# Three PSUM banks for both kinds of scores, a penalty written by ScalarE for every second head, and six batches' values made ahead of the feed-forward part

## The reference, cut to what matters

```python
# layer 0, attention; layer 1 is the same without the mask
Q = (layernorm(x) @ W_q.T) ; K = (ctx @ W_k.T) ; V = (ctx @ W_v.T)      # 16 heads of 16
scores = where(mask, Q @ K.T / sqrt(16), -1e10)                          # per head 256 x 256
x = x + tanh(g) * (softmax(scores) @ V @ W_proj.T + b_proj)
# layer 0, feed-forward: act_qdq rounds with one scale, the maximum of all of x
x = x + tanh(g) * (act_qdq(silu_q(gate) * up) @ Wd.T)
```

## Time and profile before

| | |
|---|---|
| median of three runs | 1262.97 us |
| the profiled execution | 1267.7 us (span 1266.4) |
| layer 0, attention | to about 455 us |
| feed-forward part | about 460 to 790 us |
| layer 1, attention | about 760 to 1115 us |
| experts | to the end |
| granted TensorE clock, mean | 0.98 of full speed |

### The profile page before, as it was taken

One profiled execution on the slowest core, in us unless ns is written; L12 is line 12 of the kernel. 1 busy time (PEld: TensorE's weight loads), 2 busy tenths in 40 slices (PEclk: granted clock), 3 DMA queues, 4 the chain that ended last, 5 costly groups with the idle time before them and its releaser, 6 DMA issues.

```text
span 1266.4 us, 25147 instructions
## 1 busy us (share of the span) xinstructions
PE 1188.2 (94%) x9260; PEld 877.5 (69%) x9260; DVE 892.3 (70%) x2680; ACT 709.8 (56%) x1197; POOL 480.1 (38%) x677
## 2 busy tenths in 40 slices
PE   7799999999999989999999978999999999889998
PEld 6577777777777654444458866777777777578987
DVE  4687878877788446599999846768778778642343
ACT  2356556565656538899964425666666666622221
POOL 5445434443342000166001433443643643323555
PEclk9899999999999989999999999999999999988999
DMA  7424333433331050000004643364563442147973
GB/s 188 136 62 126 106 107 89 114 111 88 115 87 54 19 176 1 1 1 1 1 25 143 184 134 105 106 169 131 154 172 112 134 129 61 52 160 250 304 193 37
DMA packets 121941, 137.23 MB, mean 108 GB/s; under 512 B 12881, under 2 KB 116427, under 8 KB 121797
## 3 DMA queue, kind: packets, MB, share of 16 engines
q1 hardware_dynamic: 111888, 125.98, 33.5%
q0 software_dynamic: 7296, 8.15, 3.5%
q10 hardware_dynamic: 2634, 1.49, 0.5%
HBM read 58.42 MB, written 27.36 MB: 68 GB/s over the span
## 4 chain that ended last, share of the span: by engine, by line
PE 72%; DVE 9%; ACT 6%; issue 6%; POOL 3%; DMA 1%; ACTq 1%; SPq 1%; another core or an unknown queue 0%; POOLq 0%; DVEq 0%
PE PS L676 14%; PE PS L477 8%; PE PS L418 7%; PE PS L461 6%; PE PS L722 6%; PE PS L437 6%; PE PS L690 4%; PE PS L509 4%; PE PS L535 4%; PE PS L464 3%; PE PS L425 3%; ACT P L846 2%; PE PS L731 2%; DVE MX L1123 2%; DVE ON L1181 2%
## 5 line engine op out<-in xcount | busy, mean ns | idle before, releaser
L846 ACT ACTIVATE P<-PS 128x512 f32<-128x512 f32 x512 | 300.0, 602 | 125.0 <-PE PS L464 75.7
L461 PE MATMUL PS<-QS,KS 99*128 99x256 bf16 x1024 | 226.7, 274 | 14.4 <-ACT P L846 13.3
L1123 DVE CUSTOM_DVE_ANT_0 MX<-PS,NQ 128x256 bf16<-128x256 f32 x512 | 191.8, 417 | 56.1 <-PE PS L437 56.1
L1126 DVE TENSOR_REDUCE NM<-PS 128x2 f32<-128x512 f32 x256 | 172.2, 684 | 64.9 <-PE PS L437 64.5
L437 PE MATMUL PS<-KS,QS 96*128 96x256 bf16 x1024 | 195.4, 274 | 5.9 <-DMA QS<-PP 2.1
L461 PEld LDWEIGHTS PS<-QS,KS 99*128 99x128 bf16 x1024 | 92.7, 99 | 61.6 <-issue 23.3
L464 PE MATMUL PS<-NK,identb 128*128 128x256 bf16 x512 | 127.9, 274 | 0.0
L477 PE MATMUL PS<-P,V 128*32 128x256 f32 x2048 | 125.5, 386 | 1.2 <-ACT P L846 1.2
L676 PE MATMUL PS<-XNT,wup 128*128 128x512 f16 x576 | 124.9, 379 | 0.0
L437 PEld LDWEIGHTS PS<-KS,QS 96*128 96x128 bf16 x1024 | 96.6, 98 | 36.8 <-issue 10.2
L676 PEld LDWEIGHTS PS<-XNT,wup 128*128 128x128 f16 x576 | 56.2, 98 | 67.4
(11 more groups left out here) (234 smaller groups left out, 2465.1 us busy)
## 6 DMA issues: line engine op xcount, KB each, us to landing
KS<-PP SPq DMA_DIRECT2D x192, 128.0 KB, 3.1
QS<-PP SPq DMA_DIRECT2D x192, 128.0 KB, 2.7
WH<-in_wex SPq DMA_DIRECT2D x16, 768.0 KB
WG<-in_wex SPq DMA_DIRECT2D x10, 768.0 KB
bufd<-bias_row SPq DMA_DIRECT2D x5, 1032.0 KB, 12.4
XB<-in_x SPq DMA_DIRECT2D x16, 256.0 KB, 3.4
CT<-in_ctxT SPq DMA_DIRECT2D x16, 256.0 KB, 3.1
x1d<-XB SPq DMA_DIRECT2D x16, 256.0 KB, 2.1
```

Source lines behind the costliest of these rows:

```text
L461: ins = tensor.matmul(o, t.KS[b % 3][0:99, h, 128 * kt:128 * kt + 128], t.QS[b % 3][0:99, h, :], start=True, stop=(L == 1))
L846: scalar.activation(t.P[i % NP_RING][:, :, :], PS[:, h % 2, :].rearrange("p (k n) -> p k n", k=2), ACT.Exp).then_inc(s_ex, 1)
L1123: ins = vector.tensor_tensor_reduce(t.MX[:, 2 * score_turn(L, b, h) + qt, :], PS[:, bk, 256 * qt:256 * qt + 256], t.NQ[b % 4][:, qt, :], - ...
L1126: ins = vector.tensor_reduce(nm[:, :, h], PS[:, bk, :].rearrange("p (t n) -> p t n", t=2), X, ALU.max, negate=True)
```

## The change

1. Banks: both kinds of scores have three banks each (scores 2, 3, 4; transposed scores 0, 1, 5), by the same turn. A transposed head waits for the exponential three before it, not two. The head outputs move from bank 4 to the odd banks.
2. Penalty, layer 0: for every odd head but head 1 of batch 0 ScalarE copies `NK` into the bank first (`act_penalty`, three heads ahead, right behind the exponential that frees the bank), and TensorE adds its two score matmuls to it. An even head gets one identity matmul of 512 columns ahead of its two.
3. Order: `pe_av` stands before the heads of its slot, `act_heads` moves one slot earlier and before the exponential.
4. Values: those of batches 3, 5, 7, 9, 11 and 13 of layer 1 are made in the last slots of layer 0 and before the feed-forward part, 24 matmuls in pieces (`BETWEEN`), most in place of warming matmuls. Their context and weights are loaded in one go (seven DMAs of 256 KB), ScalarE copies them, SP stores them to DRAM (512 KB each) and loads them back in layer 1, each at k=5 two batches ahead. In layer 1 TensorE and ScalarE skip these batches' values.
5. Several semaphores are merged, since the new ones need room.

```diff
+VPRE = (3, 5, 7, 9, 11, 13)
+BETWEEN = {(NB, 1): 1, (NB, 5): 2, (NB, 8): 2, (NB, 10): 2, (NB + 1, 4): 7}
...
-    return (2, 3, 5)[score_turn(L, b, h)]
+    return 2 + turn_of(L, b, h)
...
+def laid_first(b, h):
+    return h % 2 == 1 and (b, h) != (0, 1)
+def score_t_bank(L, b, h):
+    return (0, 1, 5)[turn_of(L, b, h)]
...
-            pe.wait_ge(s_ex, i - 1)
+            pe.wait_ge(s_ex, i - 2)
             if L == 0:
                 pe.wait_ge(s_pen, n + 1)
-            bk = h % 2
+            if L == 0 and laid_first(b, h):
+                pe.wait_ge(s_pre, i // 2)
+            bk = score_t_bank(L, b, h)
+            laid = L == 0 and laid_first(b, h)
+            if L == 0 and not laid:
+                tensor.matmul(PS[:, bk, :], identb[:, :], t.NK[b % 4][:, :, :].rearrange("p k n -> p (k n)"),
+                              start=True, stop=True)
             for kt in range(2):
-                o = PS[:, bk, 256 * kt:256 * kt + 256]
-                ins = tensor.matmul(o, t.KS[b % 3][0:99, h, 128 * kt:128 * kt + 128], t.QS[b % 3][0:99, h, :],
-                                    start=True, stop=(L == 1))
-                if L == 0:
-                    ins = tensor.matmul(o, identb[:, :], t.NK[b % 4][:, kt, :], start=False, stop=True)
+                ins = tensor.matmul(PS[:, bk, 256 * kt:256 * kt + 256], t.KS[b % 3][0:99, h, 128 * kt:128 * kt + 128],
+                                    t.QS[b % 3][0:99, h, :], start=(L == 1), stop=True, skip_group_check=(L == 0))
...
         def pe_av(L, b, hh):
-            pe.wait_ge(s_ot, 2 * n + hh)
+            bk = odd_bank(("av", n, hh), s_ot, 2 * n + hh + 1)
+            pe.wait_ge(*values_ready(L, b))
...
+        def pe_between(units):
+            for u in range(done_between[0], done_between[0] + units):
+                j, tt, k = u // 4, u // 2 % 2, u % 2
+                if u % 4 == 0:
+                    pe.wait_ge(s_mx, 16 * NB)
+                    pe.wait_ge(d_cb, 16 * (len(VPRE) + 1))
+                    pe.wait_ge(s_bv, j - 1)
+                ins = tensor.matmul(PS[:, 2 + j % 2, 256 * tt:256 * tt + 256], CTB[j][:, k, 128 * tt:128 * tt + 128],
+                                    t0.W["k"][:, k, :], start=(k == 0), stop=(k == 1))
...
         def pe_slot(L, s, k):
+            if L == 0:
+                pe_between(BETWEEN.get((s, k), 0))
+            if 0 <= s < NB and k == 9:
+                pe_av(L, s, 0)
+            if 0 <= s - 1 < NB and k == 1:
+                pe_av(L, s - 1, 1)
...
-                    if s - 2 == NB - 1:
-                        pe_warm(4, 14)
+                    if (L, s - 2) == (1, NB - 1):
+                        pe_warm(5, 14)
...
-            pe_warm(4, 6)
+            pe_between(4)
             pe.wait_ge(s_am, NB)
             pe_scale_a(0)
             pe_scale_b(0)
-            pe_warm(4, 13)
-            for i in range(NCH):
+            pe_between(6)
+            pe_ff_in(wgt, 0)
+            pe.wait_ge(s_bv, len(VPRE))
+            for i in range(1, NCH):
                 pe_ff_in(wgt, i)
...
+        def act_penalty(b, h):
+            i = 16 * b + h
+            act.wait_ge(s_pen, b + 1)
+            act.wait_ge(s_ex, i - 2)
+            scalar.activation(PS[:, score_t_bank(0, b, h), :].rearrange("p (k n) -> p k n", k=2), t0.NK[b % 4][:, :, :],
+                              ACT.Copy).then_inc(s_pre, 1)
...
         def act_slot(L, s, k):
+            if 0 <= s < NB and k == 9:
+                act_heads(L, s, 0)
+            if 0 <= s - 1 < NB and k == 1:
+                act_heads(L, s - 1, 1)
             if 0 <= s < NB:
                 act_exp(L, s, k)
+            ahead = 16 * s + k + 3
+            if L == 0 and 0 <= ahead < 16 * NB and laid_first(*divmod(ahead, 16)):
+                act_penalty(ahead // 16, ahead % 16)
...
+        def act_between(j):
+            if j == 2:
+                act.wait_ge(s_ah, 2 * NB)
+            if j >= 3:
+                act.wait_ge(d_bv[j % 3], 16 * (j // 3))
+            act.wait_ge(s_bvp, j + 1)
+            scalar.activation(VB[j % 3][:, :, :, 0:16],
+                              PS[:, 2 + j % 2, :].rearrange("p (t h r) -> p t h r", t=2, h=H), ACT.Copy).then_inc(s_bv, 1)
...
             act_high(0)
             act_high(1)
+            act_between(4)
+            act_between(5)
...
+        def sp_values(b):
+            j = VPRE.index(b)
+            for i in range(3):
+                sp.wait_ge(d_bv[i], 16 * (len(VPRE) // 3))
+            sp.wait_ge(s_ah, 2 * (NB + b - 2))
+            sync.dma_start(t1.V[b % 3][:, :, :, :].rearrange("p t h r -> p (t h r)"), vd[j]).then_inc(d_bv[j % 3], 16)
...
+            if (L, s, k) == (0, NB - 2, 6):
+                sp_between_loads()
+            if L == 0 and (s, k) in ((NB, 11), (NB + 1, 2), (NB + 1, 3), (NB + 1, 8)):
+                sp_between_store(((NB, 11), (NB + 1, 2), (NB + 1, 3), (NB + 1, 8)).index((s, k)))
+            if L == 1 and s + 2 in VPRE and k == 5:
+                sp_values(s + 2)
```

115 lines of the change are left out of this document (74 added, 41 removed).

## The result

The changed kernel takes 1248.36 us (median of four runs, 1244.62 to 1249.9), the kernel before 1262.92 in runs beside it: ratio 0.9884, 95% interval 0.9859 to 0.991. On another chip, with five runs, it was 1245.6 us and 0.9847 (0.9831 to 0.9863). So the change gives 1.2 to 1.5%, 15 to 20 us, where I forecast 31. The sign was right and the time lies in the range, but half of the forecast gain is missing.

What follows compares the result with a forecast made beforehand. TensorE, busy 94% of the span, was taken to bound the kernel. The terms -16.5 + 0.5 - 13 - 1.8 = -30.8 us, from the median 1262.97, gave 1232 us, range 1215 to 1251.

Steps and rivals of the forecast that it cites:

- Layer 0's penalty: Odd heads' penalty moved from TensorE to ScalarE: -1.1 us on the mean of 15 batches, -16.5 us, and +0.5 in the sixteenth.
- cost 0: Head outputs sharing the two odd banks: their new emptiers finish in time, cost 0; 0.1 to 0.5 us a batch if ScalarE is late.
- The place on ScalarE where it bites: Layer 0, head 5's penalty ahead of exponential 3 and QF: QF at +4.4 us, projection ends at +3.8, ON chain 0.4 later.
- my sixteenth batch: Layer 0's last stage, without scores beside it: ScalarE becomes the bound, +0.5 us.
- rival B: ScalarE's queue: new waits take half, a copy with its wait costing 0.9 us; 1250 us, chance 0.17.
- Banks in layer 1: Third bank and earlier head copy: -1.0 us on eleven batches, -0.5 on the other four, together -13 us.
- Six values: Layer 1 loses 10.4 us of TensorE work in six batches, but VectorE is next: counted 0, bounds 0 and 10.4.
- rival C: Slower, by the clock: falls in layer-0 batches, low for 5 us, 2.5 us a batch; about 1294 us, chance 0.05.
- The tail: End of layer 0: new matmuls in TensorE's pauses should hold the clock for the last output projection, -1.8 us, 0 if it falls.
- A: The values count: VectorE's slack lets the freed 1.73 us through, 10.4 us more; 1222 us, chance 0.12.
- D: It does nothing: VectorE paces both loops, so both edits free unused time; 1262 us, chance 0.04.
- the three signs that I named for being wrong: Penalty copies above 0.8 us, a loop's clock under 1.00, or TensorE waiting for the odd banks.

## Why the prediction was right or wrong, point by point

**Layer 0's penalty, -16.5 us and +0.5: 5.9 of the 16.0 came.** This is the step that failed: the term "-1.1 on the mean of 15", taken from one batch with little else in it, measured 0.54 on the mean of twelve, and the +0.5 for the last stage measured 2.05. The thirteenth batch gained more than forecast (22.51 to 20.55 us), the fifteenth stage lost 0.53. For an ordinary batch I had -0.55 from keys to the end of the queries, +0.25 to ON, -0.3 to the output projection, -0.7 to the next keys, -1.3 together; the quiet batch shows -0.46, +0.30, -0.24, -0.76, together -1.16. But I allowed 0.2 us on the mean for batches with weight preparation and took -1.1 for all fifteen. The twelve lengths of the kernel before could have warned me: they run from 24.59 to 27.08 us, so "ordinary" was the exception. Of what is missing in the twelve batches against -1.16 each (13.9 - 6.5 = 7.4 us), 3.7 lie in the three with weight transposes (3 x 1.16, and the 0.2 that they got longer) and the rest in the other nine; the part of VectorE's preparation that I cut accounts for 2.1 of it (9 x 0.23), all in three batches. What holds the rest is open; I only know that of 0.59 us added to VectorE 0.47 arrive.

Why the three batches gained nothing is half settled. I had written "cost 0" for moving the head outputs to the shared banks, with the keys' copy covered by 1.9 us of head outputs. This cover fails where a weight job shifts the turn: then the head outputs themselves are what waits for the keys' copy. The kernel with all penalties on TensorE has this wait too and is 2.0 us longer there than the kernel before (81.82 against 79.81), so it comes with banks and order, not with ScalarE's penalties, which give most of that back (80.04). Whether the shift of the turn alone makes it, no run separated: both attempts to change it brought longer waits of their own.

**The place on ScalarE where it bites** was right: the penalties of heads 5 and 7 stand ahead of copies that TensorE waits for. I counted them as worth nothing; they cost 0.31 us a batch. The copy's price was right (602 ns, 0.53 from its start at 205.25 to the next one's at 205.78; I took 0.5), and so was QF's place: it starts at 203.64, 0.6 us after the query projection. The 0.2 us for a wait before each copy did not come (5.0 us over 127), so ScalarE is busy 78% of the loop and not near 85%. The stage behind the last scores, my sixteenth batch, +0.5, has 2.05 us instead (21.25 against 19.20, at clock 0.92): there TensorE waited 2.39 us for the copy XNT, and the clock fell to 0.50 at once. With six penalties it is 19.70, with no fall. That is rival B's mechanism, and C's, in one place.

```profile
420.29 0.44 PE L700 MATMUL PS<-ident,w_nat 128*128 128x128 f32 x2 [2.39 <-ACT XNT L980]
```

**Banks in layer 1, -13 us:** 10.0 came in the two profiles (328.4 to 318.4 us from the first to the sixteenth output projection), 8.3 where neither side has a fall of the clock. An ordinary batch went from 22.81 to 22.08, 0.73 and not 1.0, the far end of the 21.8 to 22.1 that I gave. The third bank's part, 0.54, is what I read. The 0.25 that I gave to the earlier head copy did not come: the router's matmuls still wait 0.25 us for ON, at 798.21, 820.30 and 842.38.

**Six values, 0 us:** right, and for the reason given, VectorE's maxima. What I did not see is that the move is not free. Small: the stage before the last output projection of layer 0 takes 13.73 us with the pieces and 13.30 without. Larger: the waits that it opens let the clock fall. I had rival C in layer 0, at a size that outweighs everything; it came in layer 1, in the batches that I had made thin myself, at 1.6 us each, once in one profile of the changed kernel and three times in the other.

**The tail, -1.8 us:** the projection's record is 1.99 us instead of the 3.78 of the earlier trace rows. Whether for my reason stays open: it is 1.99 us in four of the seven profiles without work in the tail too, and in all twelve with such work. And the term was counted against one profile, not against the median from which I subtracted it.

**Rivals.** A is refuted: none of the six batches took 20.5 us. B describes the outcome best (1250 forecast, 1248 measured): new waits take half of layer 0. That the measured time lies in my range is B's doing, since I had drawn the range to take B in. Its mechanism, copies late for the shared banks, is there in three batches and in the stage behind the last scores; its premise, a copy with its wait at 0.9 us, is not. I gave it 0.17; the mixture of batches should have given it as much as the forecast. D is refuted by the time, but its premise is nearer than I thought: in the changed kernel all of what is added to VectorE arrives in layer 1 and four fifths in layer 0. Two of the three signs that I named for being wrong came: TensorE waits for the odd banks, and the clock of layer 1's loop is 0.99.

The Trainium skill (TensorE: Matmul & The Clock Gate, A second HAM failure mode: psum-queue depth-cycling) warns of a clock that swings when TensorE has many short idle times between groups. In the changed kernel's layer-0 loop the trace does not agree (1.00), though several of its variants have one fall there. In layer 1 it agrees for the batches without values: one at 22.08 us and 1.00, its likes at 23.7 and 0.93. I set the rule aside because of a row of the kernel before, though the change was going to alter just what that row showed.

## What to carry to other kernels

Price a change in the shortest and in the longest turn of a loop before taking a mean: what a step frees in a quiet batch may be owed to another engine in one that carries background work. Before moving work off an engine, look for what its time hides: if another engine ends last there, nothing is gained, and the pauses may cost the clock. When a buffer gets new users, check the turn for every order in which they can come, not just the usual one.

## What the runs showed of the hardware

- A fall of TensorE's granted clock to 0.50 costs an ordinary batch of layer 1 about 1.6 us (22.08 to 23.7), and the same kernel has it in different places from one execution to the next (at 967 us in one profile, at 781, 917 and 1009 in the other). In layer 1's loop, in ten profiles with six batches without values each, 26 of the 60 batches without values had one; of the sixty with values beside them, none. In eight profiles with all values in the layer there was one in 96 batches, in a batch with routing work (26.08 us at 0.93), so it is not excluded there. The counts go by the length of each batch: over 1 us more than an undisturbed one of its kind.
- Without the added reduction the clock fell in 20 of 54 batches without values, in 19 of them 6 to 8.2 us behind the output projection, where TensorE has three waits close together (0.30, 0.64 and 0.50 us in an ordinary batch of the changed kernel); with 0.6 us more of VectorE in the batch, each of the six had one. In the sixty batches with values beside them, TensorE busy some 21.8 of 22.08 us where nothing else was changed, there was none.
- ScalarE's copy from SBUF to PSUM takes 602 ns for 512 columns and 388 ns for 256, the first just what its reads from PSUM of this width take (599 ns for the exponential).
